# Router logits as extra columns of the sums, and unscaled rows in the expert queue, in a two-layer block on one core

## What is computed

```python
x = x + attn1(layernorm(x))
h0 = layernorm(x)
x2 = h0 + attention(rmsnorm(h0) * ln1_w) @ wo.T          # layer 2, before the experts
h = rmsnorm(x2) * ln2_w
logits = h @ gate_w.T                                    # 8 experts
topw, topi = top_k(softmax(logits), 2);  topw /= topw.sum()
out = sum_e topw_e * ((silu(h @ w1[e].T) * (h @ w3[e].T)) @ w2[e].T)
x = x + x2 + out
```

## Time and profile before

| | us |
|---|---|
| median of 3 runs (lowest, highest) | 1736.43 (1735.91, 1738.32) |
| the profiled execution, time | 1730.77 |
| the profiled execution, span from first to last instruction | 1729.1 |
| stage 7 starts in the span | 1212.6 |
| first and last scatter start | 1237.8, 1334.8 |
| first expert matmul | 1345.5 |

### The profile page before, as it was taken

One profiled execution on the slowest core, in us unless ns is written; L12 is line 12 of the kernel. 1 busy time (PEld: TensorE's weight loads), 2 busy tenths in 40 slices (PEclk: granted clock), 3 DMA queues, 4 the chain that ended last, 5 costly groups with the idle time before them and its releaser, 6 DMA issues. The chain is left out here.

```text
span 1729.1 us, 29571 instructions
## 1 busy us (share of the span) xinstructions
PE 1624.7 (94%) x9040; PEld 807.7 (47%) x9040; DVE 1166.1 (67%) x3195; ACT 931.3 (54%) x2069; POOL 556.0 (32%) x842
## 2 busy tenths in 40 slices
PE   7899989899999999999999999998995899999996
PEld 3367655333333333334333343332884455565554
DVE  6722788899888888888888888870685344343342
ACT  6134544166676776676676766667573333333332
POOL 3530338163515003030030300000377344444443
PEclk9999999799999999999999999999895899999999
DMA  5000000311030300303003030000378677777774
GB/s 165 1 7 19 2 1 7 62 36 28 2 62 2 62 2 1 62 2 62 2 1 62 2 62 2 1 1 1 120 234 276 122 129 130 131 130 129 129 126 71
DMA packets 252195, 105.77 MB, mean 61 GB/s; under 512 B 208064, under 2 KB 247880, under 8 KB 252040
## 3 DMA queue, kind: packets, MB, share of 16 engines
q1 hardware_dynamic: 233296, 80.62, 22.0%
q0 software_dynamic: 13392, 18.49, 6.3%
q10 hardware_dynamic: 5352, 4.76, 0.8%
HBM read 30.88 MB, written 23.67 MB: 32 GB/s over the span
## 5 line engine op out<-in xcount | busy, mean ns | idle before, releaser
L1677 ACT ACTIVATE prob<-pS 128x512 f32<-128x512 f32 (+3 forms) x1280 | 582.3, 542 | 267.5 <-PE pS L1563 176.2
L1734 DVE TENSOR_REDUCE mx<-pM 128x1 f32<-128x512 f32 x768 | 501.6, 685 | 71.3 <-PE pM L1543 68.1
L1543 PE MATMUL pM<-KT,QT 96*128 96x512 bf16 (+3 forms) x1280 | 434.1, 356 | 16.5 <-DVE mx L1734 5.5
L1559 PE MATMUL pS<-QT,KT 99*128 99x512 bf16 (+3 forms) x1280 | 422.9, 352 | 6.8 <-ACT prob L1677 1.8
L2440 PE MATMUL bank<-w13T,QKV 128*128 x568 | 257.2, 596 | 15.4 <-ACT QKV L2467 15.4
L1730 DVE CUSTOM_DVE_ANT_0 junk<-pM,mask_row 128x128 bf16<-128x128 f32 (+3 forms) x512 | 239.9, 483 | 41.7 <-PE pM L1543 41.1
L1578 PE MATMUL pO<-prob,VV 128*32 128x512 f32 (+3 forms) x2560 | 267.8, 536 | 0.0
L1543 PEld LDWEIGHTS pM<-KT,QT 96*128 96x128 bf16 x1280 | 124.5, 98 | 208.5 <-DVE mx L1734 79.1
L1468 POOL CAST mpart<-mneg 128x16 bf16<-128x16 f32 x32 | 6.8, 213 | 653.9 <-DVE mneg L1742 653.9
L1559 PEld LDWEIGHTS pS<-QT,KT 99*128 99x128 bf16 x1280 | 123.6, 97 | 184.0 <-ACT prob L1677 140.2
L2500 DVE TENSOR_TENSOR QKV<-QKV,bank 128x512 f32<-128x512 f32 x71 | 48.8, 687 | 235.5 <-issue 200.2
(11 more groups left out here) (356 smaller groups left out, 1947.3 us busy)
## 6 DMA issues: line engine op xcount, KB each, us to landing
raw<-in_ffn_w_dram SPq DMA_DIRECT2D x48, 256.0 KB, 4.0
QKV<-queue SPq DMA_DIRECT2D x71, 136.0 KB, 2.5
out_dram<-x ACTq DMA_DIRECT2D x8, 512.0 KB, 4.7
x<-_attn_hidden_states_dram SPq DMA_DIRECT2D x14, 256.0 KB, 5.5
QKV<-QKV SPq DMA_TRANSPOSE x142, 3.2
QT<-mrow SPq DMA_DIRECT2D x128, 3.0 KB
out_dram<-QKV POOLq DMA_INDIRECT x71, 3.9
wc_s<-in_attn_Wc_dram SPq DMA_DIRECT2D x1, 1024.0 KB, 8.1
```

The costliest lines, as they stand in the source:

```text
L1543: last = nc.tensor.matmul(pM[:, bank, 0:w], QT[0:ROWS, par, h, qt * P:(qt + 1) * P], KT[0:ROWS, par, 512 * part:512 * part + w], start=Tru ...
L1559: last = nc.tensor.matmul(pS[:, p % NSC, lo:512], KT[0:ROWS + 3, par, kt * P:(kt + 1) * P], QT[0:ROWS + 3, par, h, 512 * c + lo:512 * c + ...
L1677: nc.scalar.activation(prob[:, n % RING, h, lo:512], pS[:, p % NSC, lo:512], ACT.Exp, scale=SCALE).then_inc(s.head_exp, 1)
L1734: nc.vector.reduce_max(mx[:, h, qt, part:part + 1], pM[:, plan.bank[item], 0:w], AX.X).then_inc(s.unit_max, 1)
```

## The change

The router's weights are scaled and centred in stage 4 and turned there, and two more products are made. The 8 router columns of the normalised input are appended to `wqkvT`, so stage 6 projects 392 columns instead of 384; the product of `wo` and the router's weights is appended to `woT`, so `project` makes 264 columns. The sums in `attended` are then 264 columns wide and their last eight are the logits. `turn_h`, `h_out`, `logits` and `records` go. The rows enter the queue unscaled: `ln2_w` goes into the experts' first weights (`weights_out` becomes two activations with a scale for each of the 32 blocks of `w13`), the rms factor goes into the token's weights (one more small product in `choose`) and into `silu` as its scale, with one more word in the record.

`xl` gets two buffers and `normal` runs a beat ahead; `pX` has three slots of a bank each instead of four half banks. The beats go from 11 to 10: `squares`, `soften` and `choose` of group q come in beat q+1, `settle` and `scatter` in beat q+2. The weight blocks come 4 a beat in beats 1 to 6, then 8 a beat in beats 7 to 9.

```diff
-    LATE = NQ + 3
+    LATE = NQ + 2
+    SX = 3
-            per = [0, 0, 4, 4, 4, 4, 4, 4, 8, 8, 8]
+            per = [0, 4, 4, 4, 4, 4, 4, 8, 8, 8]
             for beat in range(1, LATE):                       # POOL
-                if beat >= 3:
-                    scatter(beat - 3, 0, 4)
                 if beat <= NQ:
                     root2(beat - 1)
-                if beat >= 3:
-                    scatter(beat - 3, 4, 4)
+                if beat >= 2:
+                    scatter(beat - 2, 0, 8)
             def project(i):                                   # PE
                 pe.wait_ge(s.aT_out, i + 1)
-                if i >= 2:
-                    pe.wait_ge(s.x2, 2 * i - 2)
                 for j in range(2):
+                    t = 2 * i + j
+                    if t >= SX:
+                        pe.wait_ge(s.x2, t - SX + 1)
             ...
-                    if 1 <= beat <= NQ:
-                        turn_h(2 * (beat - 1) + j)
-                    if 1 <= beat <= NQ:
-                        logits(2 * (beat - 1) + j)
-                if 2 <= beat <= NQ + 1:
+                if beat >= 2:
                     ranks(beat - 2)
                 turn_weights(ws[3 * quarter:])
             ...
+                if beat < NQ:                                 # ACT
+                    attended_out(2 * beat)
+                if beat == 0:
+                    normal(0)
+                weights_out(ws[0:quarter])
                 if 1 <= beat <= NQ:
                     squares(beat - 1)
+                if beat < NQ:
+                    attended_out(2 * beat + 1)
+                weights_out(ws[quarter:2 * quarter])
+                if beat + 1 < NQ:
+                    normal(beat + 1)
+                if 1 <= beat <= NQ:
+                    exponential(beat - 1)
                 weights_out(ws[2 * quarter:3 * quarter])
             ...
             for beat in range(LATE):                          # DVE
-                if 2 <= beat <= NQ + 1:
-                    soften(beat - 2)
-                    records(beat - 2)
-                    choose(beat - 2)
                 if beat < NQ:
                     attended(beat)
-                if 2 <= beat <= NQ + 1:
+                if beat + 1 < NQ:
+                    routed(beat + 1)
+                if 1 <= beat <= NQ:
+                    soften(beat - 1)
+                if beat >= 2:
                     settle(beat - 2)
                 if beat == 2:
                     spare_hot()
+                if 1 <= beat <= NQ:
+                    choose(beat - 1)
                 if beat < NQ:
                     residual(beat)
```

More of the change, by code:

```diff
@@ L936, in turn_weight, with output_gate @@
                                                    ident[0:rows, 0:rows])
+                    last.then_inc(s.wT_mm, 1)
+                def output_gate():
+                    pe.wait_ge(s.wT_out, 6)
+                    for m in range(C):
+                        for c in range(C):
+                            last = nc.tensor.matmul(pQK[:, 1, m * E:(m + 1) * E], raw[:, 3 + c, m * P:(m + 1) * P],
+                                                    v.gws[:, c, :], start=(c == 0), stop=(c == C - 1))
                     last.then_inc(s.wT_mm, 1)
@@ L1953, in project @@
                 pe.wait_ge(s.aT_out, i + 1)
-                if i >= 2:
-                    pe.wait_ge(s.x2, 2 * i - 2)
                 for j in range(2):
+                    t = 2 * i + j
+                    if t >= SX:
+                        pe.wait_ge(s.x2, t - SX + 1)
                     for c in range(C):
-                        last = nc.tensor.matmul(pX[:, 2 * (i % 2) + j, :], aT[:, i % 2, j, c, :], v.woT[:, c, :],
+                        last = nc.tensor.matmul(pX[:, t % SX, :], aT[:, i % 2, j, c, :], v.woT[:, c, :],
                                                 start=(c == 0), stop=(c == C - 1))
                     last.then_inc(s.proj, 1)
[L1962 to L1972, removed]
-                if i == 0:
-                    pe.wait_ge(s.gw_ready, C)
-                pe.wait_ge(s.hT_out, i + 1)
-                q = i // 2
-                if i % 2 == 0 and q >= 1:
-                    pe.wait_ge(s.soft, 2 * (q - 1) + 1)
-                if i % 2 == 0 and q >= 2:
-                    pe.wait_ge(s.place, q - 1)
-                for j in range(2):
-                    for c in range(C):
-                        last = nc.tensor.matmul(logits_at[:, 2 * (i % 2) + j, :], hT[:, i % 2, j, c, :], gws[:, c, :],
-                                                start=(c == 0), stop=(c == C - 1))
-                last.then_inc(s.logits, 1)
             def ranks(q):
@@ L2235, in route_dve @@
             nc.vector.memset(prior[:, 0, :], 0.0).then_inc(s.prior0, 1)
-            dve.wait_ge(s.ln_in, 16)
-            for c in range(C):
-                nc.vector.tensor_scalar(gws[:, c, :], v.gwT[:, c, :], ln2c[:, c:c + 1], None,
-                                        ALU.mult).then_inc(s.gw_ready, 1)
+            routed(0)
             for beat in range(LATE):
-                if 2 <= beat <= NQ + 1:
-                    soften(beat - 2)
-                    records(beat - 2)
-                    choose(beat - 2)
-                if beat == 4:
+                if beat == 3:
                     spare_out()
```

176 lines of the change are left out of this document (91 added, 85 removed).

## The result

The changed kernel takes 1752.14 us (median), 1.0089 times the kernel before, with a 95% interval of 1.0068 to 1.0111. A second set of runs gave 1750.67 us and 1.0087 (1.0065 to 1.0109). A ratio of 1.0087 is 15 us in 1736.

What follows compares the result with a forecast made beforehand. POOL, full with scatters in stage 7, was taken as the bound; +8.2 us at the end of the scatters and 0.5 elsewhere make 8.7, added to the median 1736.43: 1745.1 us, range 1735 to 1752.

Steps and rivals of the forecast that it cites:

- The bound: Stage 7: POOL, full with 64 scatters at a pitch of 1.27 us, decides when the experts start.
- The round trip: Stage 7, each group: POOL's root2 to DVE's soften and settle and back to the scatter; POOL stands still 2.45 us.
- The third rival: Stage 7: no change, with a handover of 0.2 us instead of 0.9; 0 to 3 us more, 1737 to 1739; chance 0.15.
- the first rival: Stage 7: waiting for root2 to return costs POOL nothing, POOL is full; faster, 1730 us; chance 0.11.
- Scatters that run long: Stage 7, POOL: scatters lengthened beside DVE's wide residual sums, 0.25 us a group.
- P: Stage 7: one round of the loop between POOL and DVE, the pitch of groups of eight scatters, 13.95 us.
- shorter single scatters: Stage 7, POOL's timeline: single scatters would be shorter after the change; no size given.
- The first scatter: Start of stage 7's scatters on POOL: at 1239.0 (1237.1 to 1241), 1.2 us later than before.
- The first gap: Stage 7, PE's spare_tokens before the fourth group's project: hidden unless PE is at half clock, then up to 2 us.
- The eighth group and the end: Stage 7: last group waits 1.0 us (0 to 2.5) for ranks(7), starts at 1334.1, ends at 1344.0, +8.2 us.
- Elsewhere: Outside stage 7: stage 4 0.5 us more (0 to 1.5), stage 6 under 1 us and mostly hidden, stage 8 nothing.
- PE at half clock: Stage 7: PE at 1.2 GHz sets a beat of about 15.3 us; 8 us more, 1753; chance 0.10.

Runs made afterwards that it cites:

- The first experiment: The changed kernel with DVE doing settle(b-2) ahead of soften(b-1): 1738.71 us, 1.0015 times the kernel before.
- the two experiments without it: The changed kernel with residual adding only 8 of 256 columns, 1744.81 us; the changed kernel with two small 128x16 sums on DVE ahead of each residual, 1743.72 us.

## Why the prediction was right, and where its size was off

**The bound: right.** POOL's scatters end stage 7. After the last of them the first expert matmul follows in 9.7 to 9.8 us, as the 9.76 that the prediction left alone.

**The round trip: right, in kind and size.** Forecast were 2.45 us of POOL standing still; 2.28 or 2.29 were measured, before each group from the third to the seventh. The handover to a scatter that really waits was taken from two rows as 0.9 against the 0.3 of one that follows another; from 1276.66 + 0.17 to 1277.63 it is 0.80. The third rival, which needed 0.2 there, is out. PE is no part of this loop: `ranks` of the group whose slots come at 1276.83 was over at 1270.0. The first experiment removed the wait, and the first rival's picture, POOL full, appeared in its middle groups: it needed `settle` not to wait for `soften`, as the prediction said.

**Scatters that run long: the term that was mis-sized.** The sum has 0.25 a group for them, an average over the profile before. It is 0.99 in each of the first six groups. In the kernel before, `residual` fell at another moment of the row of scatters each time, and in the first profile it lengthened only two by more than 0.1 (by 0.81 and 0.45). All together, spread over six groups, this is 0.23, so 0.25 was right for that kernel. In the changed kernel one loop ties DVE to POOL's root, so `residual` begins 0.09 to 0.11 before a scatter in six groups out of six, which is about the dearest place. This makes P: 13.95 + 0.74 here - 0.17 at the wait = 14.52, where 14.58 were measured. The loop sets five gaps, so 0.74 makes 3.7 us, as much as the forecast of stage 7 lacked in the first profile (11.8 against 8.2); in the first gap the long scatter cost nothing, as the two experiments without it show. The prediction's sign of shorter single scatters came out the other way, 1073 ns in the mean against 1018. The inference of the Trainium skill weighed against this term (SBUF — State Buffer, section "Who interferes with whom"), by which it would have been nothing, pointed the wrong way.

**The first scatter: wrong, by 1.2 in two profiles of three.** It starts 25.17 us after the start of the stage, where the kernel before had 25.22 and the forecast 26.4; in the third profile it is 26.3. The half-clock `project` came as said, but `choose(0)` was over at 1240.56, 18.15 us into the stage, where the forecast's chain has 1232.3 - 1212.58 = 19.7:

```profile
1238.96 3.48 PE L1982 MATMUL bank<-woT,turned 128*128 128x264 f32 x8
1240.37 0.19 DVE L2199 TENSOR_TENSOR QKV<-wqkvT 128x32 f32<-128x32 f32 x1
```

This error has the other sign than the one above and hid a part of it, which is luck.

**The first gap: left out.** Between the first and second group are 15.46, 0.9 over the others. PE waited 3.87 us for `spare_hot`, then `spare_tokens` ran at a granted clock of 0.50 (3.57 us for 16 products, 1.87 in the kernel before), both ahead of the fourth group's `project`, for whose sums DVE waits before it comes to the second group's `settle`:

```profile
1249.38 3.57 PE L2020 MATMUL bank<-self_f,w2T 128*128 128x1 f32 x16 [3.87 <-DVE w2T L2222]
```

The prediction named this, with up to 2 us, "in the upper bound", and left it out of the sum. Its upper bounds do not add up either: the four listed make 16.5 (1753), not 15 (1752), and these 2 are not among them. DVE's beat, given as 11, adds up to 10.0 from the terms named; nothing hung on that.

**The eighth group and the end: right in kind, too narrow.** 11.4 us after the seventh was forecast; 11.16, 13.52 and 10.99 were measured. The wait for `ranks(7)` depends on when block loads land, and varies.

The sum for the first profile, against the forecast end of scatters: 8.2 - 1.3 (first scatter) + 4.7 (six gaps of 88.36 against 83.7) - 0.2 (eighth) + 0.4 (last group, 10.3 for 9.9) = 11.8, as measured: the last scatter ends 134.99 after the start of the stage, and 123.20 in the kernel before. For the other two profiles it is 14.1 and 13.0. Added to the median of the kernel before, with the 0.3 of stage 4, these give 1748 to 1751, at the upper end of the range given.

**Elsewhere: right.** Stage 4 has 0.34 more, under the 0.5 taken, and stage 6 nothing that stands out of its variation. What is left between 12 to 14.5 us so accounted for and the 15 of the ratios is smaller than their intervals, and stays open. In the experiments too the medians fall by up to 4 us more than stage 7 does, against its mean of 145.89.

**The rival whose number fitted.** PE at half clock was said to give 1753. PE's clock did fall to 0.80 and 0.74, but moving one DVE step brought the groups from 14.58 to 11.6 apart, and two more DVE instructions brought them to 13.6. Neither takes work from PE, and the gaps stay the same at clocks from 0.62 to 0.85. PE was waiting, not waited for: the row below is in the beat shown above.

```profile
1277.15 1.09 PE L2012 MATMUL bank<-ident,raw 128*128 128x128 f32 x4 [6.28 <-ACT w13T L2084]
```

## What to carry to other kernels

When one engine both makes a value and consumes what is computed behind it, look for the loop: engine A's step, engine B's queue up to the thing that A needs next, and back. Its idle time is paid once per turn, however early the data itself was ready, and a swap of two steps in B's queue can take it off. An interference that shows as a small average in a loose schedule can fall on its worst moment in every turn once a loop locks the engines together; so size it by its worst row too, not by its mean alone. And when the first bound goes, ask what is queued behind it: here the end of the stage, where `ranks` stands behind weight blocks, took back some 4 us.

## What the runs showed of the hardware

A scatter is held up by `residual`, a sum of 128x1024 with both inputs in SBUF, only if it begins from about 0.04 to 1.07 us after it (at 0.03 and 1.12 it was not); then it ends about 2.05 us after `residual` began (once 2.14), wherever it started. Offsets and lengths in these profiles: 0.10 and 1.95, 0.29 and 1.77, 0.47 and 1.58, 0.55 and 1.50, 0.64 and 1.41, 0.85 and 1.20; the sums are 2.05 or 2.06. Scatters that began shortly before it, or 0.02 after it, took their usual 0.96 to 0.98. In one profile of the kernel before three were caught, at 0.04, 0.17 and 0.19 (2.01, 1.88 and 1.95 long), and its stage 7 was 1 us longer than in the others. The sums of `attended`, 0.43 us long with one input in PSUM, lengthened none: at 1283.60 one began 0.18 before the scatter at 1283.78, which took 0.96, and so did all others that began within such a sum (0.96 or 0.97).

The Trainium skill, SBUF — State Buffer, section "Who interferes with whom", says that a DVE instruction with two SBUF inputs contends with a GpSimd instruction that reads SBUF, and one with at most one SBUF input, outside the 2-port modes, does not. These rows agree with both halves. By its inference in the same section a tensor_tensor does not stall the making of descriptors. These scatters were lengthened all the same; they also read their row numbers from SBUF, and which of their steps is held was not measured apart.
